# Where the experts' weights are split: first product's in the experts' stage, second product's in the self-attention

## What is computed

```python
logits = jnp.einsum('bsej,bsj->bse', attn, v).reshape(-1, E)
top_logits, idx = jax.lax.top_k(logits, TOP_K)
scores = jax.nn.softmax(top_logits, axis=-1)
for e in range(E):
    h1 = x_rep @ w1[e].T              # 256 -> 2 x 704
    a, g = jnp.split(h1, 2, axis=-1)
    he = silu(a) * g @ w2[e].T        # 704 -> 256
    out = out + where(expert_ids == e, he, 0)
out = out * scores; combined = the sum of a token's two rows
```

## Time and profile before

| | us |
|---|---|
| median of 3 runs (1883.78 to 1885.42) | 1885.15 |
| the profiled execution | 1884.02 |
| its span, first to last instruction | 1882.2 |

### The profile page before, as it was taken

How to read it: one execution, slowest core, us unless ns; L and a number is a source line. 1 busy time by engine, 2 the same in 40 slices (tenths; PEclk the granted TensorE clock), 3 DMA queues, 4 the chain that set the end, 5 groups by cost and what they waited for, 6 DMA issues and landing times. The chain is left out here.

```text
span 1882.2 us, 59167 instructions
## 1 busy us (share of the span) xinstructions
PE 1736.2 (92%) x24673; PEld 1146.0 (61%) x24673; DVE 1387.1 (74%) x3579; ACT 1307.0 (69%) x1610; POOL 1293.4 (69%) x669
## 2 busy tenths in 40 slices
PE   6899999999999999999999999999778993699996
PEld 3566666666666666666666666666534672588885
DVE  7788888888888888888888888788766566544443
ACT  5588788888878888878888878888664442233332
POOL 3488888898888888898898888888652100243442
PEclk9999999999999999999999999999898785799998
DMA  8544445444445544445554545554166674688884
GB/s 274 157 119 121 128 113 156 130 127 112 131 117 151 136 129 112 131 117 146 138 132 111 132 117 142 134 138 104 51 215 203 202 236 148 241 248 254 267 245 119
DMA packets 170923, 290.83 MB, mean 155 GB/s; under 512 B 56162, under 2 KB 138466, under 8 KB 170434
## 3 DMA queue, kind: packets, MB, share of 16 engines
q1 hardware_dynamic: 163170, 276.83, 50.6%
q0 software_dynamic: 7488, 10.23, 2.7%
HBM read 169.80 MB, written 33.16 MB: 108 GB/s over the span
## 5 line engine op out<-in xcount | busy, mean ns | idle before, releaser
L420 POOL TENSOR_TENSOR pl<-pT,ph 128x1024 f16<-128x1024 f32 x416 | 881.7, 2132 | 188.4 <-ACT ph L462 188.2
L679 DVE CUSTOM_DVE_ANT_0 junk<-ring,mbias 128x804 bf16<-128x804 f32 x496 | 491.5, 991 | 155.7 <-issue 150.1
L460 ACT ACTIVATE pT<-score,small 128x1024 f32<-128x1024 f32 (+1 forms) x416 | 464.5, 1117 | 68.0 <-PE score L485 34.0
L462 ACT ACTIVATE ph<-score,small 128x1024 f16<-128x1024 f32 (+1 forms) x416 | 464.5, 1117 | 0.0
L883 PE MATMUL ring<-cp,wkp 128*128 128x402 f16 x1536 | 309.0, 338 | 10.2 <-DVE kst L758 3.3
L894 PE MATMUL ring<-wvp,cp 128*128 128x256 f16 (+1 forms) x2496 | 306.3, 274 | 2.9 <-DVE v L664 1.7
L894 PEld LDWEIGHTS ring<-wvp,cp 128*128 128x128 f16 (+1 forms) x2496 | 233.7, 99 | 78.4 <-issue 21.8
L623 POOL TENSOR_TENSOR cp<-cx,cp 128x804 f16<-128x804 f32 x128 | 252.9, 1996 | 21.5 <-ACT cp L792 21.5
L800 ACT ACTIVATE kh<-ring,small 128x402 f16<-128x402 f32 x256 | 155.2, 606 | 154.9 <-PE ring L883 154.9
L908 PE MATMUL ring<-kh,qm 32*128 32x402 f16 x992 | 253.1, 334 | 4.9 <-DVE mx L679 0.3
L507 PE MATMUL o_acc<-v,pl 128*128 128x33 f16 (+1 forms) x3328 | 240.2, 178 | 0.0
(11 more groups left out here) (243 smaller groups left out, 2098.5 us busy)
## 6 DMA issues: line engine op xcount, KB each, us to landing
cx<-in_ctxT SPq DMA_DIRECT2D x32, 1601.0 KB, 6.7
w1p<-wsp SPq DMA_DIRECT2D x24, 1408.0 KB, 8.0
kst<-kh SPq DMA_DIRECT2D x256, 100.5 KB, 2.9
msk<-in_mask SPq DMA_DIRECT2D x64, 400.2 KB, 5.5
kst<-kh SPq DMA_DIRECT2D x256, 99.6 KB, 2.5
wsp<-w_parts SPq DMA_DIRECT2D x24, 704.0 KB, 5.8
w2p<-wsp SPq DMA_DIRECT2D x24, 640.0 KB, 4.3
kst<-kl SPq DMA_DIRECT2D x128, 100.5 KB, 2.7
```

What stands on the lines that cost most here:

```text
L420: pool.tensor_tensor(pl[:, u].rearrange("p h q -> p (h q)"), pT[:, u], ph[:, u].rearrange("p h q -> p (h q)"), ALU.subtract).then_inc(pl_r ...
L460: act.activation(pT[0:n, u].rearrange("k (h a q) -> k a h q", a=2, q=S), scored, ACT.Exp, bias=lift[0:n, 0:1], scale=SSCALE)
L462: act.activation(ph[0:n, u].rearrange("k h (a q) -> k a h q", a=2), scored, ACT.Exp, bias=lift[0:n, 0:1], scale=SSCALE).then_inc(exp_done, 1)
L679: dve.tensor_tensor_reduce(junk[:, n % 2], made[:, :, 0:KW], mbias[:, j, 2 * KW * half:2 * KW * half + 2 * KW].rearrange("p (c k) -> p c k ...
```

## The change

The first product's weights are no longer split in the self-attention. Only the second product's piece of each expert stays there, so the tables hold 8 of WL, HI, LW and WS instead of 24, and wsp holds 8 pieces. In the experts' stage w1s, with three buffers, takes the float32 weights of a tile's expert straight from the input (1408 KB, as many bytes as w1p took before). ACT writes the high part of a third of them (high_w1: 2 x 512, 2 x 512 and 2 x 384 elements on 128 partitions) and DVE the low part (low_w1), and up(i, u) waits for its own third. Which thirds are made after which step stands in SPLITS. keep_y moves from DVE, mid tile, to ACT, after high_product(i, 2); its constant factor goes into wslot in keep_rows. The clearing of he moves from DVE to POOL.

```diff
+STAGES = 3
+PIECES = [(i, u) for i in range(NT) for u in range(UN)]
+        SPLITS[i, u] = [q for q in PIECES[at:at + (COUNT[i] if i else 2)] if q[0] < i + WB]
...
-                 "LW15 MC13 RM14 R8 SU7 NU1 LW16 R9 MC14 R10 RM15 SU8 SU9 SU10 RC4 RC5 MC15 LW17 O11 RC6 RC7 O12 LW18 "
+                 "SU4 RM13 R6 SU5 SU6 O7 MC12 MC13 RM14 LW5 O8 MC14 RM15 LW6 O9 MC15 RC0 O10 O11 LW7 RC1 RC2 RC3 O12 "
...
+                    def load_first(i):
+                        j = i % STAGES
+                        if i >= STAGES:
+                            sp.wait_ge(w_low, E + UN * (i - STAGES + 1))
+                        sp.dma_start(w1s[:, j], a["w1T"][expert(i)].rearrange("o (c p) f -> p (o c) f", p=P)).then_inc(w1_in[j], 16)
...
-                    for j in range(2):
-                        sp.wait_ge(w_out[j], 16 * (E * PIECES // 2))
-                    sp.wait_ge(te_ready, 1)
+                    sp.wait_ge(te_ready, 1)
+                    load_first(0)
+                    for j in range(2):
+                        sp.wait_ge(w_out[j], 16 * (E // 2))
                     for i in range(NT):
-                        load(i, bass.ds(e, 1))
+                        if i + 1 < NT:
+                            load_first(i + 1)
+                        load_second(i)
...
+                    pool.memset(he[:], 0.0).then_inc(he_clear, 1)
...
-                    dve.memset(he[:], 0.0).then_inc(he_clear, 1)
...
-                        dve.tensor_tensor(wslot[:, lo:hi], low, wslot[:, lo:hi], ALU.add).then_inc(rows_ready, 1)
+                        step(dve.tensor_tensor(wslot[:, lo:hi], low, wslot[:, lo:hi], ALU.add))
+                        dve.tensor_scalar(wslot[:, lo:hi], wslot[:, lo:hi], 1.0 / (VSCALE * WSCALE * WSCALE), None, ALU.mult).then_inc(rows_ready, 1)
...
+                    def low_w1(i, u):
+                        dve.wait_ge(w_high, E + UN * i + u + 1)
+                        j, part = i % STAGES, W1_PARTS[u]
+                        dve.scalar_tensor_tensor(w1p[:, i % WB, :, 1, part], w1s[:, j, :, part], WSCALE, w1p[:, i % WB, :, 0, part], ALU.mult, ALU.subtract).then_inc(w_low, 1)
...
+                    def high_w1(i, u):
+                        j, part = i % STAGES, W1_PARTS[u]
+                        act.wait_ge(w1_in[j], 16 * (i // STAGES) + 16)
+                        after(act, ag_done, UN * (i - WB) + u + 1)
+                        act.activation(w1p[:, i % WB, :, 0, part], w1s[:, j, :, part], ACT.Copy, scale=WSCALE).then_inc(w_high, 1)
+
+                    def keep_y(i):
+                        act.wait_ge(rows_ready, 1 if UPTO[i + 1] <= SOON else 2)
+                        act.wait_ge(y_done, i + 1)
+                        after(act, sc_done, 16 * UPTO[max(i - 1, 0)])
+                        for half in range(COUNT[i]):
+                            h = UPTO[i] + half
+                            act.activation(ys[:, i % 2, half, :], s_ps[:, i % 2, D * half:D * half + D], ACT.Copy,
+                                           scale=wslot[:, h:h + 1]).then_inc(y_kept, 1)
...
                         for u in range(UN):
+                            some = SPLITS[i, u]
                             silu(i, u)
+                            for q, n in some[0:1]:
+                                high_w1(q, n)
                             high_product(i, u)
                             if u == 0 and i + 1 < NT:
                                 high_rows(i + 1)
+                            for q, n in some[1:]:
+                                high_w1(q, n)
+                            if u == 2 and i > 0:
+                                keep_y(i - 1)
+                    keep_y(NT - 1)
...
+                        pe.wait_ge(w_low, E + g + 1)
```

More of the change, by code:

```diff
@@ L75 @@
 WP = 2 * F
+STAGES = 3
+W1_PARTS = [slice(4 * P * u, min(4 * P * u + 4 * P, WP)) for u in range(UN)]
+PIECES = [(i, u) for i in range(NT) for u in range(UN)]
+SPLITS = {}
+for i in range(NT):
+    for u in range(UN):
+        at = UN + sum(len(s) for s in SPLITS.values())
+        SPLITS[i, u] = [q for q in PIECES[at:at + (COUNT[i] if i else 2)] if q[0] < i + WB]
 HOT = 4
@@ L988, in load_whole @@
                     def load_whole(q):
[L990 removed]
+                        j = q % 2
                         after(sp, w_low, q - 1)
[L992 to L998 removed]
+                        sp.dma_start(w_whole[:, j, 0:(FT - 1) * D].rearrange("p (t d) -> p t d", d=D),
+                                     a["w2T"][q, 0:(FT - 1) * P].rearrange("(t p) d -> p t d", p=P)).then_inc(w_in[j], 16)
+                        sp.dma_start(w_whole[:, j, (FT - 1) * D:WP],
+                                     a["w2T"][q, (FT - 1) * P:F].rearrange("r (h f) -> (r h) f", h=2)).then_inc(w_in[j], 16)
                     for kind, n in SELF_SP:
@@ L1243, in _ @@
                         elif kind == "HI":
-                            e, k, j = n // PIECES, n % PIECES, n % 2
-                            act.wait_ge(w_in[j], 16 * sum(1 if q % PIECES < DC else 2 for q in range(j, n + 1, 2)))
+                            j = n % 2
+                            act.wait_ge(w_in[j], 32 * (n // 2) + 32)
                             after(act, w_out[j], 16 * (n // 2))
@@ L1422, in program @@
             iota_in = sem("iota_in")
-            w1_in, w2_in = ([sem(f"{n}{j}") for j in range(WB)] for n in ("w1_in", "w2_in"))
+            w1_in, w2_in = ([sem(f"{n}{j}") for j in range(c)] for n, c in (("w1_in", STAGES), ("w2_in", WB)))
             he_clear = sem("he_clear")
@@ L1443, in _, with expert, load_second @@
                         sp.dma_start(dst, src).then_inc(iota_in, 16)
-                    def load(i, e):
+                    def expert(i):
+                        h = UPTO[i]
+                        return bass.ds(sp.value_load(tei[0:1, h:h + 1], min_val=0, max_val=E - 1), 1)
+                    def load_first(i):
[3 more added lines that the diff above has]
+                        sp.dma_start(w1s[:, j], a["w1T"][expert(i)].rearrange("o (c p) f -> p (o c) f", p=P)).then_inc(w1_in[j], 16)
+                    def load_second(i):
                         j = i % WB
-                        after(sp, ag_done, UN * (i - WB + 1))
-                        sp.dma_start(w1p[:, j].rearrange("p c z f -> p c (z f)"),
-                                     wsp[e, 0:DC].rearrange("o c p z f -> p (o c) (z f)")).then_inc(w1_in[j], 16)
                         after(sp, y_done, i - WB + 1)
-                        whole = wsp[e, DC].rearrange("o p z f -> (o p) z f")
+                        whole = wsp[expert(i)].rearrange("o p z f -> (o p) z f")
                         sp.dma_start(w2p[:, j, :, 0:FT - 1].rearrange("p z t d -> p z (t d)"), whole[:, :, 0:(FT - 1) * D]).then_inc(w2_in[j], 16)
@@ L1651, in gates @@
                                               ALU.mult).then_inc(he_done, 1)
-                    def keep_y(i):
-                        dve.wait_ge(y_done, i + 1)
-                        after(dve, sc_done, 16 * UPTO[max(i - 1, 0)])
-                        for half in range(COUNT[i]):
-                            h = UPTO[i] + half
-                            dve.tensor_scalar(ys[:, i % 2, half, :], s_ps[:, i % 2, D * half:D * half + D], wslot[:, h:h + 1],
-                                              1.0 / (VSCALE * WSCALE * WSCALE), ALU.mult, ALU.mult).then_inc(y_kept, 1)
                     route()
@@ L1669, in _ @@
                     keep_rows(SOON, NH, 1)
+                    low_w1(0, 0)
                     low_rows(0)
+                    low_w1(0, 1)
+                    low_w1(0, 2)
                     for i in range(NT):
@@ L1674, in _ @@
                             low_product(i - 1, 2)
+                            for q, n in SPLITS[i - 1, 2]:
+                                low_w1(q, n)
                         gates(i, 1)
@@ L1678, in _ @@
                             low_rows(i + 1)
-                        if i > 0:
-                            keep_y(i - 1)
+                        for q, n in SPLITS[i, 0]:
+                            low_w1(q, n)
                         gates(i, 2)
                         low_product(i, 1)
+                        for q, n in SPLITS[i, 1]:
+                            low_w1(q, n)
                     low_product(NT - 1, 2)
-                    keep_y(NT - 1)
                 @block.scalar
```

33 lines of the change are left out of this document (15 added, 18 removed), and 40 rows, old and new, of tables (SELF_ACT, SELF_DVE, SELF_PE, SELF_SP).

## The result

| | before | after |
|---|---|---|
| median of 7 runs each (us) | 1885.42 (1883.78 to 1890.46) | 1874.07 (1868.42 to 1877.32) |
| ratio after / before, 95% interval | | 0.9929 (0.9911 to 0.9946) |
| span of the profiled execution | 1882.2 | 1874.1 |
| last router copy of the self-attention, start | 1575.42 | 1552.92 |
| te_ready (tei written), start | 1609.46 | 1584.12 |

The ratio is estimated from all runs, not from the two medians, whose quotient is 0.9940. So the change is 0.6 to 0.7% faster, 11 to 13 us, and its median lies 1 us from the forecast of 1875. But the reasons given for that number did not hold, and its closeness is in part luck: the experts' stage lost 7 us less than I said, and in this pair of profiles the self-attention gained 9 us less. The first figure is firm to some 3 us, the second isn't, as the experiments show. Most of what follows is about why.

A forecast was written before the change was run, and what follows sets the result against it. PE bounds the experts' stage; the line through all engines bounds the self-attention. Terms -34 - 0.6 + 4.4 + 17 + 2.6 + 0.5 = -10.1 us take the profiled execution to 1873.9; forecast median 1875 us, range 1858 to 1890.

The forecast's parts named there:

- self-attention and routing (te_ready): Self-attention without 16 of 24 pieces: -34 us (bounds 12 and 48); routing without DVE's clearing of he: -0.6 us.
- start (te_ready to first high product): Start of the experts' tiles: splits and hand-overs behind the first load +2.4 us, splits during tile 0 +2 us: +4.4.
- rows come late: Experts' tiles: later keep_y delays scatter and gathers, rounds 33.56 us against PE's 30.89, seven rounds: +17 us.
- end and last tile: End of the experts' stage: ACT writes rows behind its last high product, +2.6 us; the last tile itself +0.5.
- 6 us more for the clock: Self-attention: part of the 34 us gain, added for the clock to the 28 us that DVE loses.
- The price of a split: Experts' stage: ACT 1.05 us for 1024 elements, 0.84 for 768; DVE 1.22 and 0.95.
- (a): Experts' tiles: rows come in time, each round's spare absorbs the delay; sum -27 us, 1858 us; chance 0.18.
- (b): Whole kernel: gain and loss cancel, self-attention gaining only 24 us with the clock; 1885 us; chance 0.13.
- (c): Experts' stage: waits lower PE's clock, 11 us in all, with a 20 us self-attention gain; 1900 us; chance 0.12.
- (d): Experts' stage: POOL's scatter and gather issues held up by splits, 2.4 us a round, 17 in all; 1892 us; chance 0.05.
- What would show it: Profile signs: self-attention 30 to 38 us earlier, higher clock there, rounds 33 to 34 us, end about 3 us longer.
- w_low: Experts' tiles: PE waiting for this split would mean the prediction is wrong, with ACT or DVE the bound.

The follow-up runs named there:

- e5: Kernel before, with 14 of 16 first-product weight pieces split only for 16 of 1408 elements; order, waits and transfers unchanged: ratio to before 0.9992.
- e6: Changed kernel, with the self-attention tables of before minus the 16 pieces' steps and nothing else moved: ratio to before 1.0034.
- e11: Kernel before, with the change's self-attention order and all 24 pieces, placed so that no split waits long for load or store: ratio to before 0.9922.
- e4: Kernel before, with only keep_y moved to ACT after high_product(i, 2); all splits stay in the self-attention: ratio to before 1.0062.
- e1: Changed kernel, with keep_y(i - 1) before silu(i, 2) on ACT instead of after high_product(i, 2): ratio to before 0.9866.
- e2: Changed kernel, with low_product(i - 1, 2) before gates(i, 0) on DVE instead of behind it: ratio to before 0.9966.
- e8: Kernel before, with the change's self-attention order and all 24 pieces put back, stores queued behind a query step's 12 transfers: ratio to before 1.0060.
- e3: Changed kernel, with keep_y back on DVE, ahead of gates(i, 2) and behind the splits of (i, 0): ratio to before 0.9874.

## Why the prediction held, term by term

| term | said | profile | |
|---|---|---|---|
| self-attention and routing (te_ready) | -34.6 | -25.3 | reason wrong, size open |
| start (te_ready to first high product) | +4.4 | +4.9 | right |
| tiles: "rows come late" | +17 | +9.4 | another cause |
| end and last tile | +3.1 | +2.9 | right |
| sum | -10.1 | -8.1 | |

**Self-attention.** The -25.3 is one pair of profiles. The ratio says more: the kernel is 11 to 13 us faster although its experts' stage is 16 to 17 us longer, which leaves a gain of 28 to 31 us ahead of that stage. So -34.6 was too large by some 4 to 7 us, but the way to it was wrong. The step that failed is "I take 28 us, what DVE loses, because DVE is the fuller of the two engines". The size of the removed work was no guide: e5 takes most of it away for nothing. The diff's new tables are 20 us of gain with the pieces gone (e6 against the change) and 14 with them in (e11); the pieces gone are worth about 10 in the old order (e6; in its profile te_ready is 6.6 us earlier). That order and work together came near 34 us is luck. I had read the changed order as a consequence of the missing pieces. The signs were there: PE's longest waits were for normalisations and maxima, steps of the main line. The "6 us more for the clock" was wrong too: 2 x (1 - clock) x time gives 67 us at the lower level before, 70 after, where another execution of the code of before has 94 (e4).

**The price of a split** was right to 1% on both engines (said 1.05, 0.84, 1.22, 0.95 us). keep_y on ACT takes 0.472 us, not the 0.593 of a step with factor and offset: my nearest row was too dear by 0.12, some 5 us of ACT time that nothing waits for.

**Rows come late.** The mechanism is real and the sum was done rightly; one summand was not. Of the two waits for rows in the kernel after, the one of 3.5 us (at 1747.8) has its like in unchanged stages: 1.7 us before, 2.9 in e5, 3.6 in e11. Here is the round of the other, 0.52 us, with the weights' load (L1458), scatters (L1501) and gathers (L1492):

```profile
1759.20 0.60 PE L1787 MATMUL ring<-ident,xs 128*128 128x128 f32 x4
```

```profile
1779.80 0.39 SPq L1458 DMA_DIRECT2D w1s<-in_w1T  x1
1781.72 1.62 POOL L1501 DMA_INDIRECT acc_d<-ys,to_row  x1 [7.88 <-ACT ys L1726]
...
1785.52 1.62 POOL L1492 DMA_INDIRECT xs<-xn_d,from_row  x1 [0.30 <-issue]
1787.44 0.98 POOL L1492 DMA_INDIRECT xs<-xn_d,from_row  x1 [0.30 <-issue]
1791.50 0.66 PE L1787 MATMUL o_acc<-ident,xs 128*128 128x128 f32 x4 [0.52 <-DMA xs<-xn_d,from_row]
```

Turning to ys written is 22.25 us (said 22.48), ys to scatter 0.27 (0.27), scatter to last gather 5.72 (5.12), and gather to rows turned 4.06, where I had put 5.69 from a single landing. That is 32.3 us instead of 33.56. The medians of all gathers, issue to landing, in the kernels before, after and e1 (1640 to 1840 us):

```profile
xs<-xn_d,from_row POOLq DMA_INDIRECT x32, 5.4
```

```profile
xs<-xn_d,from_row POOLq DMA_INDIRECT x29, 4.2
```

```profile
xs<-xn_d,from_row POOLq DMA_INDIRECT x29, 5.4
```

Before, the last gather went out 2.7 us behind the load of 1408 KB; such a load takes 7.9 us in the median, so it was still under way. After, it goes out 7.6 us behind its load (1779.80); such a load takes 6.9 in the median, and this one is over. A later keep_y thus shortened the landing that I had held fixed. e4, with the same late keep_y and no splits, has 3.9. The Trainium skill (DMA: Bandwidth & Descriptors, "Issuing engines are not separate DMA queues") says that transfers started by different engines run on the same 16 DMA engines and interleave; the kernel after agrees, where the 18 gathers whose issue ended while such a load was in flight land after 4.6 us in the median, and the other 11 after 3.4. In e2 it isn't so (4.1 and 4.7). That the overlap is the reason is thus likely, not shown.

What did cost in the tiles was not in the sum: keep_y ahead of silu(i + 1, 0) on ACT, 0.7 us a round, 5.1 us in all (9.4 - 4.3); late rows are 2.3 (4.0 - 1.7), no more than the unchanged stage scatters by (3.8 in e5, none in e8, 3.6 in e11); the first round and the rest are 2.0. I had asked who waits for keep_y's result, and not who waits for what stands behind keep_y. In e2 rounds like the forecast's, 33.6 to 35.0 us, came about in four of seven.

**The rivals.** (a), rows in time, was nearer than my forecast for the rounds, but its 1858 needed the full gain of 34 us and the whole 17 us of rows away. (b)'s gain of 24 us is what this pair of profiles shows, less than the ratio does; its loss was too large. (c) was right in kind and small in size. From 1618 to 1850 us the clock fell once, right behind the wait of 3.5 us for rows:

```profile
1748.20:1751.60 3.40, 3.40 (x30) 3.15 (x29) 0.06 (x1) 1.08 (x3) 1.59 (x2) 0.50 1.02 316
```

3.4 us at half the clock cost 1.7 us, once and not in every round. In e2 it fell behind two of its waits for rows (2.3 us each) and not behind the others, of 0.7 to 2.8 us. (d) was there too, though the average hides it: 39 scatter issues took 1.617 us before and 1.653 after. In the kernel after a gather's issue takes 1.60 to 1.84 us in the 7 cases in which it runs into a split on DVE, and at most 1.02 in the 26 others. One such case stands in the round above, and it is the 0.6 us by which scatter to last gather grew (5.72 against 5.12): the gather of 1785.52, issued within

```profile
1785.04 1.21 DVE L1651 SCALAR_TENSOR_TENSOR w1p<-w1s,w1p 128x1024 f16<-128x1024 f32 x1
```

So the argument that the split's price per element shows no sign of this did not hold. Scatter issues beside a split average 1.68 us (28), others 1.59 (11), and none passes 2 us in the kernel after.

**What would show it**, as I had listed it: the end about 3 us longer (2.9) is right; first matmul 2.4 us later after te_ready (3.4, of which the landing is 0.7) is near. Wrong are PE waiting for rows in one tile of three (two tiles in all), rounds of 33 to 34 (31.6), last step 30 to 38 us earlier (22.5 in this pair of profiles), a higher clock there (0.80 against 0.83) and a clock of 1.00 in all later tiles. PE also waited once for w_low, which I had named as a sign of being wrong. That the total was right to 1 us under this is luck: a gain too large by 4 to 7 us and a loss too large by 7.

## What to carry to other kernels

When a change removes side work from a stage whose order is a hand-made table, cost the new order and the removed work apart: run the old order without the work, and the new order with it. When a step moves on an in-order engine, list what stands behind its new place and who waits for that, not only who waits for the step. And a latency in a loop with transfers is no constant: the median landing of the gathers was 3.9 to 5.4 us from kernel to kernel here, probably by what else was in flight, so give it a range from many rows. The same holds for a stage read from a single profile.

## What was unexpected of the hardware

- A GpSimd issue of an indirect transfer gets longer when it meets a split on DVE, by 0.6 us for a gather in the change. With keep_y back on DVE (e3) the 27 scatter issues that meet a split average 2.35 us and the 12 others 1.59, and one takes twice its usual time:

```profile
1660.98 3.21 POOL L1501 DMA_INDIRECT acc_d<-ys,to_row  x1 [0.31 <-issue]
```

  It isn't the split alone: in the kernel before, of the gathers of 1640 to 1840 us the five issued within 0.22 us of the start of a low product on DVE take 1.25 to 1.51 us, the 26 others at most 1.09.
- Taking 20 us of work off DVE and 16 off ACT in a stage of 200 us left PE's idle time at 29.8 us (e5), against 32.4 and 33.2 in two executions with all the work. e5's mean clock was 0.77, below the 0.83 of the kernel before, but e4 has 0.77 as well, with all the work, so the lower clock can't be put down to the edit.
- The same code had a self-attention of 197.5 us (clock 0.83) in one profile and 205.0 (0.77, e4) in another, with 32.4 and 33.2 us of idle time. PE is busy 171.8 us instead of 165.1, with 94 us at the lower level instead of 67. A single profile of this stage is good to some 7 us, no better.
